# A decoder layer on one core: the cross-attention stage laid out six slots apart instead of seven

## What is computed

```python
x = ln(x + attn(x))                 # causal self attention, relu on Q, K, V, own layer norm
x = ln(x + xattn(x, ctx))           # cross attention to 64 context tokens of 96 channels
x = ln(x + ffn(x))                  # two blocks: causal attention, then a mixture of 8 experts, top 2

def xattn(x, y, pad_mask):          # the stage that the change is about
    q = (x @ Wq.T) by heads; k, v = (y @ Wkv.T) by heads
    attn = where(pad_mask[:, None, :, None], q * d ** -0.5 @ k.T, -1e9)
    return softmax(attn) @ v
```

## Time and profile before

| what | value |
|---|---|
| median of 3 runs | 1417.39 us |
| lowest, highest | 1410.66, 1418.76 us |
| the profiled execution's own time | 1422.69 us |
| its span, first to last instruction | 1421.0 us |
| mean granted TensorE clock | 0.905 of 2.4 GHz |
| PE, DVE, ACT, POOL busy | 1238.5, 931.7, 778.4, 688.4 us |

### The profile page before, as it was taken

One profiled execution on the slowest core, in us unless ns is written; L12 is line 12 of the kernel. 1 busy time (PEld: TensorE's weight loads), 2 busy tenths in 40 slices (PEclk: granted clock), 3 DMA queues, 4 the chain that ended last, 5 costly groups with the idle time before them and its releaser, 6 DMA issues. The chain is left out here.

```text
span 1421.0 us, 29988 instructions
## 1 busy us (share of the span) xinstructions
PE 1238.5 (87%) x9702; PEld 995.4 (70%) x9702; DVE 931.7 (66%) x2772; ACT 778.4 (55%) x1591; POOL 688.4 (48%) x1233
## 2 busy tenths in 40 slices
PE   3999999988889699999996399992899999999997
PEld 2777777766666477777774388891667777768886
DVE  7689999876666778888873211112888888744553
ACT  1466677655554366666662255550466666655443
POOL 4355655653221157777776000004576676445554
PEclk9999999977785799999995599995699999979999
DMA  5878774334555454555520477763555555435774
GB/s 112 238 221 235 215 221 119 94 96 135 148 153 135 106 133 123 132 138 138 132 62 31 113 216 211 220 183 93 156 143 150 148 137 144 114 104 158 204 205 116
DMA packets 206511, 210.77 MB, mean 148 GB/s; under 512 B 44819, under 2 KB 158995, under 8 KB 206356
## 3 DMA queue, kind: packets, MB, share of 16 engines
q1 hardware_dynamic: 179760, 185.66, 48.3%
q10 hardware_dynamic: 22500, 14.81, 3.9%
q0 software_dynamic: 4096, 8.40, 2.1%
HBM read 121.84 MB, written 84.41 MB: 145 GB/s over the span
## 5 line engine op out<-in xcount | busy, mean ns | idle before, releaser
L1141 POOL TENSOR_SCALAR_AFFINE_SELECT probs<-probs 128x256 f32<-128x256 f32 (+1 forms) x576 | 281.7, 494 | 245.5 <-ACT probs L829 241.5
L829 ACT ACTIVATE probs<-weights 128x512 f32<-128x512 f32 x448 | 265.0, 598 | 120.5 <-PE weights L639 84.6
L985 DVE TENSOR_REDUCE negmax<-scores 128x4 f32<-128x512 f32 x384 | 260.9, 685 | 70.7 <-PE scores L587 58.9
L587 PE MATMUL scores<-keys,queries 128*128 128x512 f32 (+1 forms) x384 | 188.5, 498 | 7.7 <-DMA queries<-zeros 3.8
L829 ACT ACTIVATE probs<-weights,keybias 128x512 f32<-128x512 f32 x192 | 131.8, 688 | 71.5 <-PE weights L639 51.6
L639 PE MATMUL weights<-queries,keys 104*128 104x256 f32 x768 | 161.4, 294 | 0.3 <-issue 0.3
L639 PEld LDWEIGHTS weights<-queries,keys 104*128 104x128 f32 x768 | 142.6, 198 | 21.7 <-issue 3.2
L1227 POOL DMA_INDIRECT out_room<-expert_rows,y_index x64 | 63.7, 995 | 192.4 <-POOLq L1593 179.8
L989 DVE TENSOR_REDUCE negmax<-scores 128x2 f32<-128x512 f32 (+1 forms) x192 | 131.1, 685 | 30.1 <-PE scores L593 20.6
L644 PEld LDWEIGHTS weights<-queries,keys 104*128 104x128 f32 x768 | 117.8, 201 | 14.6 <-ACT probs L829 4.6
L644 PE MATMUL weights<-queries,keys 104*128 104x128 f32 x768 | 113.5, 273 | 4.0 <-ACT probs L829 4.0
(11 more groups left out here) (254 smaller groups left out, 2770.8 us busy)
## 6 DMA issues: line engine op xcount, KB each, us to landing
windows<-parts SPq DMA_DIRECT2D x192, 192.0 KB
queries<-windows SPq DMA_DIRECT2D x64, 384.0 KB
keys<-windows SPq DMA_DIRECT2D x192, 96.0 KB
hidden_room<-in_m_w SPq DMA_DIRECT2D x71, 256.0 KB, 2.7
out_room<-in_m_w SPq DMA_DIRECT2D x71, 256.0 KB, 3.2
routed_rows<-zeros SPq DMA_DIRECT2D x64, 256.0 KB, 3.5
windows<-parts ACTq DMA_DIRECT2D x64, 120.0 KB
xin<-routed_rows SPq DMA_DIRECT2D x39, 128.0 KB, 3.2
```

The source lines that it names most:

```text
L587: i = pe.matmul(bank[:], queries[0:rows, s, t * P:(t + 1) * P], keys[0:rows, s::S4, half * P:(half + 1) * P], start=True, stop=True)
L829: act.activation(probs[:, n % RING], weight_banks[n % 2][:], ACT.Exp, scale=SCALE, **bias).then_inc(exp_done.sem, 1)
L985: i = dve.tensor_reduce(most[:, part, s, :], bank[:].rearrange("p (a k) -> p a k", k=P), AX.X, ALU.max, negate=True)
L1141: pool.affine_select(out=block, in_=block, compare_op=ALU.is_ge, fill=0.0, base=0, pattern=[[0, heads], [1, P]], channel_multiplier=-1).th ...
```

## The change

Ctx items follow every six slots. The loading of a ctx item's keys and queries by SP (sp_stack) stands five slots ahead of its scores instead of eight. Its second products, and all that is placed relative to them (values, outputs, resid, store, pool_last), stand one slot earlier. Self and ffn items keep their numbers.

```diff
-    stack = -8
+    stack = {"self": -8, "ffn": -8, "ctx": -5}
...
-SLOTS = {"self": 12, "ffn": 12, "ctx": 7}
-ATTEND = {"self": 17, "ffn": 17, "ctx": 10}
+SLOTS = {"self": 12, "ffn": 12, "ctx": 6}
+ATTEND = {"self": 17, "ffn": 17, "ctx": 9}
...
-            at = first_slot[g - 1] + units[g - 1].n + (3 if units[g - 1].kind == "ctx" else 0) if g % (3 * B) else 0
+            at = first_slot[g - 1] + SLOTS[units[g - 1].kind] if g % (3 * B) else 0
...
-                at = max(at, first_slot[g - LANES] + before.attend + before.n - 1 - AT.stack)
+                at = max(at, first_slot[g - LANES] + before.attend + before.n - 1 - AT.stack[U.kind])
...
-            return combined + spread + ((AT.fetch - (6 if U.kind == "ctx" else 0), 2, sp_fetch), (AT.stack, 1, sp_stack),
+            return combined + spread + ((AT.fetch - (6 if U.kind == "ctx" else 0), 2, sp_fetch), (AT.stack[U.kind], 1, sp_stack),
...
-            relay = ((AT.stack, 0, dve_relay),) if g in relaid else ()
+            relay = ((AT.stack[U.kind], 0, dve_relay),) if g in relaid else ()
```

## The result

| | before | after |
|---|---|---|
| median | 1418.08 us (4 runs, 1410.66 to 1419.10) | 1451.76 us (4 runs, 1445.64 to 1454.77) |
| profiled execution, its span | 1422.69, 1421.0 us | 1454.68, 1452.9 us |
| mean granted clock | 0.905 | 0.890 |

The ratio is 1.0245 (95% interval 1.0201 to 1.029): 34 us slower. The sign was right, the size was not: +15 forecast, and 1451.8 lies above the range.

What follows compares the result with a forecast made beforehand. A ring over three engines bounds ctx periods at full clock, PE at 1.2 GHz. 13 periods x 1.1 = 14.3 us, plus 0.7 at the seam, gave +15.0 on 1417.39: 1432 us, range 1409 to 1445.

Steps and rivals of the forecast that it cites:

- The ring over L769, the exponential and the maxima: Ctx stage before, full clock: a once-per-item loop over three engines, 7.92 us, with L769's 2.11 us on ACT its largest term.
- Steps 1 to 6: Ctx stage after, full clock: one round from maxima to maxima through ACT, PE and DVE, 9.46 us against 8.00.
- DVE's tail: DVE's row from last maximum to next maxima: 1.75 us becomes 3.12, with L960, L964, L965 and L891 (1.37) between.
- The slow period: Ctx period at 1.2 GHz, bound by PE: taken as 11.9 us after the change, bounds 11.5 and 13.3.
- The mix of the two levels: Ctx periods weighted by time, 44% at low clock: 10.40 us against 9.35; leaning towards 0.70 clock, +1.1 per item taken.
- The issue of L769: ACT's four DMA issues directly behind L758, ahead of the fourth exponential: taken to hold ACT for 2.15 us.
- Rival C: Clock stays at 0.50 for the ctx stage: 2.7 us per item, +35 us, 1452 us; chance 0.09.
- A: L769 hides behind PE's products and PE comes to its own bound: -8 us, 1409, down to 1400; chance 0.14.
- B: One ctx stall replaces another, within half a microsecond per item: 0 to +10 us, say 1422; chance 0.22.
- D: Keys land 2 us beyond the bound, PE's scores wait for DMA: period 10.4 us, about 1433; chance 0.07.
- The seam: Before item 32, SP's spread stands ahead of item 31's stack: 0 to 2.1 us, 0.7 taken.

Runs made afterwards that it cites:

- e8: Kernel before (seven slots) with the second of the four second products of each ctx item computed four times; 0.9898 to before, 1402.79 us.
- e10: Changed kernel with the third second product of each ctx item computed six times, where PE waits for L1026; 1.0085 to before, 1428.35 us.
- e1: Changed kernel with seven slots and second products at 10 as before, only the keys' load five slots ahead; 1.004 to before.
- e7: Changed kernel with the third second product of each ctx item computed four times, where PE waits for L1026; 1.0141 to before.
- e12: Changed kernel with the fourth second product computed four times, in the middle of slot 0, where PE does not wait; 1.0259 to before.
- e3: Changed kernel with ACT's spread (L769) one slot later, behind the fourth exponential, the second L815 and L800; 1.0213 to before.

## Why the prediction was right in sign and wrong in size

- **What bounds the kernel.** The ring over L769, the exponential and the maxima at full clock was put at 7.92 us; e8 shows it at 7.91 and 7.92. The reading of the two levels, a fast period on a ring and a slow one on PE, held for the seven slots.
- **Steps 1 to 6, the new ring.** 9.46 us forecast, 9.19 to 9.49 in e10 at a clock of 1.00. That it came so near is partly luck, since two terms were off against each other. The fourth exponential was put 3.53 us behind the maxima; in the period from 398.36 in e10 it starts after 2.81. The first issue of L769 stands 0.92 behind the maxima and not 1.38, since it starts 0.33 before L758 does (399.28 and 399.61) and not 0.13 behind it, and the four hold ACT for 1.89 and not 2.15. DVE's tail from the last maximum to the maxima took 3.43 (394.93 to 398.36), not 3.12. L964 alone is 0.65 long after and 0.41 before, now with POOL's L1182 running beside it, which no run tested by itself. At full clock the order costs 9.20 - 7.91 = 1.29 us per item.
- **The slow period.** Taken at 11.9, as before the change, with bounds 11.5 and 13.3; measured 12.33 at a clock of 0.50. The row of 11.91 held other work, as the prediction said. e1, in the seven-slot order, has a period wholly at 0.50 that takes 11.10 (PE busy 10.75), in which the maxima wait 0.35 us for L1026. In the changed kernel PE is busy 10.78 of 12.33 and they wait 1.33. So DVE's tail costs about 1.2 us at the low level too, where the forecast's middle value put nothing; that the value was too high to begin with hid most of it.
- **The mix of the two levels: here it failed.** I took the clock as before, "an unchanged clock", and leaned only a little towards 0.70, for +1.1 us per item and a period of 10 to 10.8; it was 11.63. The stage ran at 0.60, so 80% of the time at the low level. The same formula with what was measured gives 1/(0.20/9.20 + 0.80/12.33) = 11.5 us against 11.63. At the unchanged share it gives 1/(0.56/9.20 + 0.44/12.33) = 10.36. So of the 2.44 us per item, 1.17 are the order, for which 1.05 was forecast, and 1.27 are the clock. The model was right and the share in it was not. The prediction itself computed 3.2 us of PE idle per fast period in place of 1.7, said that this would cost clock, and then priced that at 0.05 us per item. By the model the clock was worth about half of the loss. The filled kernels give a smaller part: e8 and e10, with the stage at 0.95 and 0.97, still differ by 25.6 us (5 of them behind the stage) of the 34, which leaves 8 for the clock. A quarter to a half is what can be said. e7, e10 and e8 show that the clock is a cause here and not only a symptom: work was added, nothing taken away, and 16, 23 and 14 us went. That activity releases the low clock, as the Trainium skill has it in "TensorE: Matmul & The Clock Gate", "Part 1: The HAM clock gate", is what these three show; e12 adds that the place of the work decides whether it pays.
- **The issue of L769, taken as fixed.** Each of the five times that the changed kernel began a period of this stage at the high level, or mostly at it, L769 took 2.75 to 3.26 us and the clock fell behind it. In e10, eight periods with L769 at 1.8 us kept a clock of 1.00, and the two with 3.03 and 2.57 us dropped to 0.85 and 0.84; in e7 one with 1.81 us dropped as well, to 0.67. So the clock may have fallen in the changed kernel for the order's own 3 us of idle time or for the longer issues on top of it. No run separates the two, and a part of what e7 and e10 gained may be that their issues were mostly short.
- **Rival C** (the clock stays down, 1452 us, given 0.09) came closest, with 1451.8. It was right in kind, though the clock went to 0.60 and not to 0.50, so that its number is met to 0.2 us is luck. Its reason against itself, that PE is 96% busy at the low level, was the mistake: in the changed kernel that share is 87% (10.78 of 12.33).
- **A** fell: no period of the stretch was under 11.0 us, and none of four other six-slot orders was faster than the kernel before. (Its mix comes to 8.71, not 8.73.) **B** fell with 2.44 us per item. **D** fell for this stretch: e1 has the late load alone, at 1.004, and no L582 matmul waits for it between 340 and 440 us in either kernel. At the ends of the stage it was there, where the prediction saw it as hidden. In the changed kernel scores of early ctx items wait 1.06 and 1.15 us for the keys' DMA (321.29 and 332.50), and once at the seam to the ffn items, 0.56 us at 483.84; in e1 it is 1.57 us at 310.56 and 2.20 at 457.10, in the kernel before never. The seam's 0.7 us stands against +1.5 for the last three items, clock included.
- **What stays open.** e3 shows that ACT's issue alone was not the binding term while the clock was low; that it is part of the ring at full clock rests on e10's timeline, not on an edit that took it out. Each period and clock is read from one execution per kernel. That six slots could be made faster than seven by a better order was not shown either way.

## What to carry to other kernels

Where TensorE's clock is seen at both levels in a stage, work out the period at either level and then the share of time at each; the share is a term with its own bounds, and here a schedule that added PE idle time moved it as much as the ring. A shorter distance in slots gives nothing by itself: count for each shared bank and each in-order queue what now stands between the producer and the consumer. An issue of DMAs on a compute engine's queue has no fixed length either. Where a short wait in each period seems to bring the clock down, repeating a matmul in front of that wait is a cheap test of it, and here a gain of 1% (e8).

## What the runs showed that was not expected

- The changed kernel reached 1428 us with ten extra matmuls per item and the kernel before 1403 us with six: at these two orders, the amount of work and the time went in opposite directions.
- The four DMA issues of L769 take 1.8 us in the slow periods of the kernel before and 2.03 to 2.38 in its fast ones, and once 3.12 (from 313.05). In the changed kernel they take 1.8 us or, five times in this stage, 2.75 to 3.26, with SP's own load starting 0.33 to 0.52 us behind them and not 0.8 or more. That nearness alone does not decide it: in e10 SP starts 0.43 us behind in nearly every period, and L769 is at 1.8 us in most of them and at 3.03 and 2.57 in two; in e8 it is at 3.05 and 3.20 in two, with SP's load 2.5 us ahead. What makes the difference was not settled.
